# An RNN and an LSTM side by side on TensorE: input products summed in the gates' own PSUM banks

## The reference

```
RNN:  r_t = tanh(x_t Wx0 + b0 + r_(t-1) Wh0),  r_(-1) = cond
x1_t = x_t + r_t
LSTM: a_t = x1_t Wx1 + b1 + h_(t-1) Wh1,  h_(-1) = cond, c_(-1) = 0
      i, f, o = sigmoid, g = tanh of a_t's four quarters
      c_t = f * c_(t-1) + i * g,   h_t = o * tanh(c_t)
x2_t = x1_t + h_t
```

## Time and profile before

| | |
|---|---|
| median of 3 runs | 2756.93 us (2755.39 to 2757.35) |
| the profiled execution | 2757.16 us, its span 2755.4 us |
| TensorE, mean granted clock | 0.976 of 2.4 GHz |
| busy share of the span | TensorE 92%, weight loads 67%, VectorE 56%, ScalarE 47%, GpSimd 8% |
| recurrences | from 10 to about 1214 us of the span |

### The profile page before, as it was taken

How to read it: one execution, slowest core, us unless ns; L and a number is a source line. 1 busy time by engine, 2 the same in 40 slices (tenths; PEclk the granted TensorE clock), 3 DMA queues, 4 the chain that set the end, 5 groups by cost and what they waited for, 6 DMA issues and landing times.

```text
span 2755.4 us, 94115 instructions
## 1 busy us (share of the span) xinstructions
PE 2537.0 (92%) x40180; PEld 1836.1 (67%) x40180; DVE 1534.4 (56%) x6279; ACT 1301.7 (47%) x3954; POOL 211.9 (8%) x225
## 2 busy tenths in 40 slices
PE   8999999999999999964488999989989899899899
PEld 6888888888888888842254654646646456465466
DVE  4666666666666666645464555545544546455530
ACT  2444444444444444424446456465464654655542
POOL 0000000000000000001010111111111111011101
PEclk9999999999999999986789999999999999999999
DMA  4000000000000000000001001010010200100110
GB/s 166 12 12 12 12 10 12 11 11 12 12 12 12 10 12 10 10 21 16 1 20 66 1 27 66 27 66 1 27 66 6 87 1 27 66 1 25 57 65 16
DMA packets 94822, 75.68 MB, mean 27 GB/s; under 512 B 72885, under 2 KB 84789, under 8 KB 89541
## 3 DMA queue, kind: packets, MB, share of 16 engines
q1 hardware_dynamic: 91764, 67.14, 7.9%
q10 hardware_dynamic: 2640, 2.53, 0.3%
HBM read 61.22 MB, written 8.44 MB: 25 GB/s over the span
## 4 chain that ended last, share of the span: by engine, by line
PE 40%; ACT 7%; DVE 5%; issue 3%; POOL 0%; DMA 0%; POOLq 0%; ACTq 0%; SPq 0%; DVEq 0%
PE bank L548 12%; PE bank L533 11%; PE bank L735 4%; PE bank L727 4%; ACT pexp L1278 4%; PE bank L636 2%; PE bank L581 1%; PE bank L623 1%; PE bank L565 1%; PE bank L687 1%; PE bank L608 1%; ACT pexp L1208 1%; PE bank L647 1%; DVE big L979 1%; ACT hidden L1190 1%
## 5 line engine op out<-in xcount | busy, mean ns | idle before, releaser
L124 PE MATMUL psFI<-wh,RH 128*8 128x128 f32 x8192 | 319.7, 274 | 6.4 <-DVE RH L237 5.9
L124 PE MATMUL psOR<-wh,RH 128*16 128x128 f32 (+2 forms) x8384 | 322.0, 272 | 0.3
L276 ACT ACTIVATE sFI<-FIT 128x32 f32<-128x32 f32 x512 | 120.4, 235 | 383.0 <-DVE FIT L223 383.0
L223 DVE STREAM_TRANSPOSE FIT<-psFI 128x128 f32<-128x128 f32 x512 | 162.6, 317 | 241.0 <-PE psFI L124 240.9
L1278 ACT ACTIVATE pexp<-bank 128x1024 f32<-128x1024 f32 x256 | 242.0, 1022 | 46.4 <-PE bank L623 46.4
L533 PE MATMUL bank<-x3T,ew 128*128 128x512 f32 x512 | 241.2, 596 | 12.2 <-ACT hidden L1190 6.7
L548 PEld LDWEIGHTS bank<-ew,hidden 128*128 128x128 f32 x1024 | 193.9, 190 | 76.7 <-issue 54.6
L548 PE MATMUL bank<-ew,hidden 128*128 128x256 f32 x1024 | 239.9, 380 | 0.0
L119 PE MATMUL psFI<-xw,pick 128*104 128x128 f32 x1024 | 238.8, 315 | 0.0
L124 PEld LDWEIGHTS psFI<-wh,RH 128*8 128x8 f32 x8192 | 171.7, 88 | 80.5 <-DVE RH L237 46.1
L119 PE MATMUL psOR<-xw,pick 128*112 128x128 f32 (+2 forms) x1048 | 223.6, 295 | 0.0
(11 more groups left out here) (240 smaller groups left out, 4358.1 us busy)
## 6 DMA issues: line engine op xcount, KB each, us to landing
ew<-in_ew SPq DMA_DIRECT2D x32, 1024.0 KB, 8.7
xc<-in_xT SPq DMA_DIRECT2D x32, 128.0 KB, 2.3
x_scratch<-x2c SPq DMA_DIRECT2D x32, 128.0 KB, 3.4
z1T<-x_scratch SPq DMA_DIRECT2D x8, 512.0 KB, 3.9
ada<-ada_scratch SPq DMA_DIRECT2D x8, 512.0 KB, 4.9
out_x<-x SPq DMA_DIRECT2D x8, 512.0 KB, 3.2
W_wf<-in_wf SPq DMA_DIRECT2D x2, 1024.0 KB
W_sw<-in_sw SPq DMA_DIRECT2D x2, 1024.0 KB
```

What stands on the lines that cost most here:

```text
L124: last = pe.matmul(bank[32 * j:32 * j + width, :], state(k), R.wh[:, k, j, cols], start=False, stop=k == KC - 1, tile_position=(0, 32 * j) ...
L223: dve.transpose(flat(R.FIT), R.psFI).then_inc(sem["fiT"], 1)
L276: act.activation(R.sFI[:, :, :, 1].rearrange("p g (k b) -> p (g k) b", k=KC), R.FIT[:, :, 0:NB], ACT.Sigmoid).then_inc(sem["sFI"], 1)
```

## The change

- **Own banks.** psX, psY, xw and pick go. psFI, psG and psOR get two buffers each; a bank of psFI or psG holds four slots, one of psOR two. ScalarE copies the bias into a bank (`bias_of_group`, `bias_of_pair`); the input products of the four (two) slots add to it over all 32 partitions of a strip; then each slot's products of the state add to their own 8 (16) partitions.
- **Wider stationary operands.** To reach partitions 8s to 8s+7, the state's operand is 8(s+1) columns wide and ends with the slot's state. What the earlier columns add falls on slots that have been read already. The states lie in `Hs`, a ring of five of 8 columns, for FI and G, and in `RH`, with r and h of a slot side by side, for O and R (16 or 32 columns wide). So VectorE writes h twice: `hL` into Hs, then `hR` into RH.
- **x for two recurrences.** `XX` holds x_t for the RNN and, beside it, x1 of 8 steps before for the LSTM's O gate. The host leaves room in it (chunks of 256 KB for 128), and VectorE writes x1 there (`xx`), in addition to x1c.
- **LAG is 8**: 520 slots, 8 of them without the LSTM.
- **Order.** On TensorE a slot now begins with the products of FI and G, then O and R (waiting for `tR` and `hR`), then eight input products of a later bank: for s = 0 and 3 O and R's, for s = 1 FI's, for s = 2 G's. On ScalarE the bias copy stands behind tanh(R). On VectorE `hR` stands between `hL` and R's transpose; L249 and L252 go, the `xx` add comes.
- **Start.** Six matmuls of zeros open the banks; a first sigmoid on ScalarE stands ahead of the loop. wx0 and wx1 are one array `wx`, loaded in two slices, and wh0 and wh1 one array `wh`; the start states come on SP's queue, three loads for two; three x chunks are loaded ahead for two. `TOTAL` has 37 semaphores for 33.

```diff
-    LAG = 12
...
+    LAG = 8
+    SLOTS = T + LAG
...
-            def inject(bank, i, cols, width):
-                reach = 96 + width
-                pe.matmul(bank[0:reach, :], R.pick[:, i % 4, 0:reach], R.xw[(i // 4) % 2][:, cols], start=True, stop=False, skip_group_check=True)
...
+            def inputs_of_pair(m):
+                if m >= PAIRS:
+                    return
+                i = 2 * m
+                pe.wait_ge(sem["bOR"], m + 1)
+                if rnn(i) and i % CH == 0:
+                    pe.wait_ge(*x_in(i // CH))
+                if lstm(i):
+                    pe.wait_ge(sem["xx"], (i - LAG) // 4 + 1)
+                x = inputs(i, 2)
+                output_and_rnn(R.psOR[m % 2], i, lambda k: x[:, k, :], 32, R.wx).then_inc(sem["XX"], 1)
+
+            def inputs_of_group(g, bank, cols, seeded, raises=None):
+                q = g - FIRST
+                if not 0 <= q < PIECES:
+                    return
+                pe.wait_ge(sem[seeded], q + 1)
+                pe.wait_ge(sem["x1"], q + 1)
+                if q == 0:
+                    pe.wait_ge(sem["ld_lstm"], 32)
+                x = piece_of(R.x1, q)
...
+            pe.wait_ge(sem["zeroed"], 1)
+            for bank in R.psOR + R.psFI + R.psG:
+                last = pe.matmul(bank, R.zero[:, :], R.zero[:, 0:bank.shape[1]], start=True, stop=True)
+            last.then_inc(sem["opened"], 1)
...
-                    h = lambda k: before[:, k, H_STATE]
-                    products(R.psFI, h, NB, F_I).then_inc(sem["FI"], 1)
-                    products(R.psG, h, NB, G_).then_inc(sem["G"], 1)
+                    end, width = single_at(i - 1) + NB, NB * (s + 1)
+                    h = lambda k: R.Hs[:, k, end - width:end]
+                    products(R.psFI[g % 2], h, width, R.wh, F_I).then_inc(sem["FI"], 1)
+                    products(R.psG[g % 2], h, width, R.wh, G_).then_inc(sem["G"], 1)
...
+                if n > 0:
+                    pe.wait_ge(sem["hR"], n)
+                end, width = pair_at(i - 1) + 2 * NB, 2 * NB * (i % 2 + 1)
+                output_and_rnn(R.psOR[(i // 2) % 2], i, lambda k: R.RH[:, k, end - width:end], width, R.wh).then_inc(sem["OR"], 1)
+                if s == 0:
+                    inputs_of_pair(2 * g + 1)
+                elif s == 1:
+                    inputs_of_group(g + 1, R.psFI, F_I, "bFI")
+                elif s == 2:
+                    inputs_of_group(g + 1, R.psG, G_, "bG", "X1")
                 else:
-                    last = products(psOR[:, 0:64], both, 2 * NB, O_)
-                last.then_inc(sem["OR"], 1)
+                    inputs_of_pair(2 * g + 2)
...
-                    dve.tensor_tensor(R.RH[:, turn, :, H_STATE], R.oT[:, :, NB:2 * NB], R.tC[:, :, :], ALU.mult).then_inc(sem["hL"], 1)
+                    o = R.oT[:, :, at_pair + NB:at_pair + 2 * NB]
+                    dve.tensor_tensor(h_alone(i), o, R.tC[:, :, :], ALU.mult).then_inc(sem["hL"], 1)
+                    dve.tensor_tensor(h_of(i), o, R.tC[:, :, :], ALU.mult).then_inc(sem["hR"], 1)
...
+                    dve.tensor_tensor(by_step(piece_of(R.x1, q)), halves(inputs(4 * q, 4))[:, :, :, 0, :], four_slots(4 * q, 0), ALU.add).then_inc(sem["x1"], 1)
...
+                    dve.tensor_tensor(halves(inputs(to, 4))[:, :, :, 1, :], halves(inputs(4 * q, 4))[:, :, :, 0, :], four_slots(4 * q, 0), ALU.add).then_inc(sem["xx"], 1)
...
+            def bias_of_pair(m):
+
+                if m < PAIRS:
+                    act.copy(R.psOR[m % 2], R.bias[:, O_R]).then_inc(sem["bOR"], 1)
+
+            def bias_of_group(g, bank, cols, raises):
+                if 0 <= g - FIRST < PIECES:
+                    act.copy(bank[g % 2], R.bias[:, cols]).then_inc(sem[raises], 1)
...
+                if s == 0:
+                    bias_of_group(g + 1, R.psFI, F_I, "bFI")
+                elif s == 1:
+                    bias_of_group(g + 1, R.psG, G_, "bG")
+                elif s == 2:
+                    bias_of_pair(2 * g + 2)
+                else:
+                    if lstm(i):
+                        act.wait_ge(sem["oT"], n + 1)
+                    bias_of_pair(2 * g + 3)
...
-            sp.dma_start(R.xc[0][:, :, :], A["xT"][0]).then_inc(sem["x_in_0"], 16)
-            sp.dma_start(R.wx0[:, :, :, :], A["wx0"]).then_inc(sem["ld_wx0"], 16)
-            sp.dma_start(R.pick[:, :, :], A["pick"]).then_inc(sem["ld_pick"], 16)
-            sp.dma_start(R.RH[:, LAG - 1, :, H_STATE], A["condP"]).then_inc(sem["ld_h"], 16)
-            sp.dma_start(R.xc[1][:, :, :], A["xT"][1]).then_inc(sem["x_in_1"], 16)
+            sp.dma_start(R.XX[0][:, :, :], A["xT"][0]).then_inc(sem["x_in_0"], 16)
+            sp.dma_start(R.wx[:, :, :, R_], A["wx"][:, :, :, R_]).then_inc(sem["ld_wx0"], 16)
+            sp.dma_start(r_of(-1), A["condP"]).then_inc(sem["ld_r"], 16)
+            sp.dma_start(h_of(LAG - 1), A["condP"]).then_inc(sem["ld_h"], 16)
+            sp.dma_start(h_alone(LAG - 1), A["condP"]).then_inc(sem["ld_h"], 16)
+            for c in (1, 2):
+                sp.dma_start(R.XX[c][:, :, :], A["xT"][c]).then_inc(sem[f"x_in_{c}"], 16)
```

More of the change, by code:

```diff
@@ L95, in __init__ @@
         self.tC = sb("tC", [P, KC, NB])
-        self.psFI, self.psG, self.psOR = ps("psFI", 128), ps("psG", 64), [ps(f"psOR{i}", 128) for i in range(2)]
-        self.psX, self.psY = [ps(f"psX{i}", D) for i in range(2)], ps("psY", 64)
+        self.psFI, self.psG, self.psOR = ([ps(f"{n}{i}", w) for i in range(2)] for n, w in (("psFI", 128), ("psG", 64), ("psOR", 128)))
         self.sem = {n: mem.enter_context(nc.semaphore(n)) for n in self.TOTAL}
 def recurrences(nc, R, A, W, x2_dram):
-    sem, LAG, PIECES = R.sem, R.LAG, T // 4
-    SLOTS = T + LAG
+    sem, LAG, SLOTS, PIECES = R.sem, R.LAG, R.SLOTS, T // 4
+    GROUPS, PAIRS, FIRST = SLOTS // 4, SLOTS // 2, R.LAG // 4
     rnn = lambda i: i < T
     lstm = lambda i: i >= LAG
-    rows = lambda j: slice(32 * j, 32 * j + 32)
     flat = lambda t: t[:, :, :].rearrange("p k b -> p (k b)")
@@ L136, in _, with output_and_rnn @@
[L136 to L141, removed]
+            def output_and_rnn(psOR, i, state, width, weights):
+                if lstm(i) and rnn(i):
+                    return products(psOR, state, width, weights, O_R)
+                if rnn(i):
+                    return products(psOR[:, 64:128], state, width, weights, R_)
+                return products(psOR[:, 0:64], state, width, weights, O_)
@@ L161, in _ @@
[L161 to L169, removed]
-                if lstm(i):
-                    if n:
-                        pe.wait_ge(sem["fiT"], n)
-                    if s == 0:
-                        pe.wait_ge(sem["E1"], g - LAG // 4 + 1)
-                    inject(R.psFI, i, F_I, NB)
-                    if n:
-                        pe.wait_ge(sem["gT"], n)
-                    inject(R.psG, i, G_, NB)
@@ L197, in _ @@
                 if 0 < i <= T:
                     pe.wait_ge(sem["tR"], i)
-                both = lambda k: before[:, k, :]
-                if lstm(i) and rnn(i):
-                    last = products(psOR, both, 2 * NB, O_R)
-                elif rnn(i):
-                    last = products(psOR[:, 64:128], lambda k: before[:, k, R_STATE], NB, R_)
-                else:
-                    last = products(psOR[:, 0:64], both, 2 * NB, O_)
-                last.then_inc(sem["OR"], 1)
+                if n > 0:
+                    pe.wait_ge(sem["hR"], n)
@@ L1480 @@
     figo = lambda a: np.stack([a[..., n * D:(n + 1) * D].reshape(*a.shape[:-1], 4, D // 4) for n in (1, 0, 3, 2)], axis=-2).reshape(*a.shape[:-1], 4, D)
-    row, col = np.arange(P)[:, None], np.arange(P)[None, :]
-    pick = np.stack([(row // 32 == col // 32) & (row % 32 == NB * t + col % NB) & (col % 32 < 2 * NB) for t in range(4)], axis=1).astype(np.float32)
     strips = lambda a: a.reshape(*a.shape[:-1], 4, D // 4)
```

170 lines of the change are left out of this document (79 added, 91 removed).

## The result

The changed kernel takes 2736.36 us (median of four runs, 2735.61 to 2738.55), the kernel before 2756.16 beside it (2754.9 to 2757.35). The ratio is 0.993, with an interval of 0.9912 to 0.9947: faster, by 20 us where 21.4 were forecast.

The account below looks back on a forecast made before the run. TensorE was taken as last in two of four slots, the LSTM's state chain otherwise; -22.5 + 5.6 - 6.2 + 1.3 + 0.4 = -21.4 us from 2757.16 gave 2735.8 (2735.5 in terms of the median), range 2723 to 2750.

Parts of the forecast that it names:

- TensorE last in two of four slots: Steady slots: without psY's products all fall to the chain's 2.255 us from 2.300, over 499 steps: -22.5 us.
- The wider loads: FI's first load, bare on the chain, costs mean 11 ns more over 511 steps: +5.6 us, bounds 0 and twice this.
- LAG and the front: Start: four fewer slots of RNN alone bring FI's first load from 27.30 to 21.1: -6.2 us.
- The stall: Steps from 27.30 to 38.51: 4.3 us lost, unexplained, left standing at 0; it may go or double.
- The cold slots: First LSTM slots find TensorE at 1.2 GHz; one and a half at 0.87 us: +1.3, bounds 0 and 3.5.
- The second multiply: VectorE's hR ahead of R's transpose: RT and tanh(R) 0.09 to 0.18 us later, hidden by reserves, cost 0.
- rival C: VectorE between hL and RT: hR and ScalarE's copy delay O and R past the reserves, +51 us, 2786; chance 0.06.
- The bias copy: ScalarE behind tanh(R): one PSUM copy per slot, about 0.28 us (0.22 to 0.59), hidden, cost taken as 0.
- Rival B: TensorE: FI's 16 weight loads all stand bare, 0.18 us a slot, giving 2822 us; chance 0.03.
- Rival A: TensorE idles at slot heads and its clock falls to 1.2 GHz in half the slots: +218 us, 2953; chance 0.04.
- The end: Before the next block: 37 semaphores for 33 drained one after another, at most 1.1 us, taken as +0.4.
- Rival D: The chain itself lengthens by 0.045 us and eats the gain, the front's part is eaten too: 2757; chance 0.05.

Follow-up runs that it names:

- e9: Kernel before, with psY's products left out altogether from the third group of steps on: 2733.56 us, ratio 0.9919.
- e1: Kernel before, with psY's products cut from eight matmuls a group to one: 2746.86 us, ratio 0.996.
- e3: Changed kernel with the stationary operands of FI's and G's state products 8 columns wide in every slot: 2729.45 us, ratio 0.9898.
- e2: Changed kernel with LAG back to 12 from 8, nothing else: 2738.99 us, ratio 0.9927.
- e4: Changed kernel with the later blocks' 21 weight loads issued one for each chunk of x, not all at the start: 2732.25 us, ratio 0.9906.
- e10: Kernel before, with the later blocks' weight loads issued one for each chunk of x: 2754.56 us, ratio 0.999.
- e11: Changed kernel with R's start state loaded first on ScalarE's queue and TensorE's wait for the LSTM's moved to its first slot: 2739.05 us.
- e5: Changed kernel with three more unread state multiplies on VectorE between hR and R's transpose: 2751.29 us, ratio 0.9977.
- e6: Changed kernel with six more unread state multiplies on VectorE between hR and R's transpose: 2882.33 us, ratio 1.0455.
- e7: Changed kernel with an extra unread 128-column ScalarE copy into SBUF ahead of each bias copy: 2738.03 us, ratio 0.9929.
- e8: Changed kernel with each block of eight input products cut to one matmul of 8 columns: 2771.74 us (three runs of four), ratio 1.0043.

## Why the prediction was right

The bound, the size of the main term and the reserves were read rightly, and that decided it. That the sum comes within 0.2 us of the difference of the spans (-21.4 and -21.6) is in part luck: the front gave 1.4 us more than was put down and the steps 1.1 less, and the two nearly cancel. Against the medians the sum is 1.6 us too large (19.8 measured).

**TensorE last in two of four slots (-22.5).** Right, and shown by e9: without psY's products the kernel before has the chain's step in all four slots. e1 gives half for half.

**The wider loads (+5.6).** Right in kind, low in size: e3 gives 12 ns a step by the steps' medians, 15 by the four slots shown, where 11 were charged, 6 to 7 us in all. It lies near the one exposed load of FI and not near the doubled bound, so G's loads pay little. The two terms give -16.9 by the prediction and 499 x 0.033 = -16.5 by the trace.

**LAG and the front (-6.2).** The front gave 7.6. R's first load came at 10.20 for 10.93, 0.7 earlier, just outside the +-0.6 allowed for it. The eight slots took 9.47 us (to 19.67) where 10.2 were put down. e2 gives the four slots of the lag 6.7 at the front, of which 2.4 come back in the steps.

**The stall (0, "may go or double").** It grew by 2.2 us. This is the term that was mis-sized, and the prediction had left it without a mechanism. There is one: e4 and e10 show that the later blocks' loads cause it, and the traces have TensorE's instructions arriving late beside them. With a front 7.6 us shorter the same loads fall on more of the LSTM's slots, so some of each microsecond won at the front comes back; e11 shows it alone (2.3 won, 4.0 lost in the steps), e2 the other way round (6.7 lost, 2.4 returned).

**The cold slots (+1.3).** The place was wrong. The first LSTM slot is not cold: 22.03 - 19.67 = 2.36 us. The step from 26.83 to 30.08, 3.25 us, is, after the stall had kept TensorE idle for 2.56 us. The cost is part of the 6.8 lost, and goes with the stall in e4, where 20 to 40 us is granted 1.00.

**The second multiply, rival C.** Cost 0 was right, by e3's step of 2.254. Beyond the multiply's own 0.09, the spare ahead of O and R's loads was put at 0.07 to 0.16 us and the next reserve at 0.14, together 0.21 to 0.30; e5 and e6 give 0.15 to 0.16 and 0.10, together some 0.26, and e6 confirms the price beyond it.

**The bias copy.** Estimated at 0.28 us, it takes 0.26, and e7 shows as much again to spare.

**Rival B, bare weight loads.** Four slots of 9.07 us leave no room for 15 more bare loads (0.16 us a slot). The rule of the Trainium skill, TensorE: Matmul & The Clock Gate, "What overlaps and what doesn't", that a load overlaps matmuls in flight only where its row group differs, doesn't hold for these column strips.

**Rival A, the clock.** It didn't come, but 0.04 was too low for how near it lay. The tail was taken as a control for 0.52 us of idle time; the change leaves 0.80 to 0.91, and at 0.93 to 1.02 (e8) the clock was lost time and again. What keeps it here is the input products behind O and R, which the prediction counted only as a load to be fitted in; the end of e2, where they stop, lost it too. The Trainium skill, TensorE: Matmul & The Clock Gate, "A second HAM failure mode: psum-queue depth-cycling", has a kernel that cycles banks with short idle stretches lose its clock repeatedly; the changed kernel cycles banks and didn't in 1125 us, e8, with the same banks and less work, did.

**The end (+0.4)** was +0.3. **Rival D** falls with e9 and the step of 2.267.

The best version that the experiments gave is the changed kernel with the paced loads: 2732.25 us, ratio 0.9906, some 4 us below the change (5.7 by the steps); the early start adds nothing to it.

## What to carry to other kernels

An engine that is busy all the time isn't the bound of every slot: compare the steps of single slots, ask which of them begin with idle time, and price the change only for those that don't. A gain at the front of a kernel that shares its first microseconds with bulk loads is partly given back, so pace the loads before shortening the front. And before taking work off TensorE, ask whether that work is what keeps its clock: here the version with the fewest products was 35 us slower.

## What the runs showed of the hardware

- A matmul on one strip of 32 columns keeps TensorE about as long as four side by side: 0.21 us for two records in e1, 0.22 for eight in the kernel before, and the step at that slot stays at 2.35.
- Weight loads behind other products cost next to nothing, up to 32 columns (4 ns a step at most in e3); only the first after a wait is on the chain, 88 ns for 8 columns and 109 for 32.
- The clock stayed at 2.4 GHz with 0.80 to 0.91 us of idle time in each slot of 2.27, and was lost in five stretches of 3 to 21 us, besides the long one at the start, with 0.93 to 1.02 (e8).
- While the transfer engines were 0.88 to 0.99 busy, TensorE's loads stood for 2.56 us waiting for nothing that the profile's waits show, and from 13.87 to 22.73 us no instruction packet started on q8; at 0.02 (e4) they didn't stand, and one started every 4.0 to 5.3 us.
- ScalarE copies 128 columns into PSUM in 0.26 us, against 0.59 for 512 out of PSUM.
